# Sums of attention weights as three bf16 parts, and feed-forward matrices parked in DRAM

## The reference, cut to what matters

```python
dot = einsum('bqhd,bkhd->bhqk', q, k)
att = softmax(dot)                      # exp(dot - max) / sum over keys
out = einsum('bhqk,bkhd->bqhd', att, v) @ w_u
```

## Time and profile before

| | us |
|---|---|
| median of 3 runs (lowest, highest) | 3775.59 (3775.01, 3776.57) |
| the profiled execution | 3777.26 |
| its span in the trace | 3775.5 |
| PE busy | 3594.2 (95%) |
| DVE busy | 2860.7 (76%) |
| ACT busy | 2330.0 (62%) |
| POOL busy | 449.4 (12%) |

### The profile page before, as it was taken

The page is one execution under the profiler, slowest core; times in us unless marked ns, Lnnn a source line. Parts: engine busy times, 40 slices in busy tenths (PEclk is TensorE's granted clock), DMA queues, the critical chain, the costliest instruction groups (busy, mean ns, idle before and its releaser), DMA issues.

```text
span 3775.5 us, 66359 instructions
## 1 busy us (share of the span) xinstructions
PE 3594.2 (95%) x24697; PEld 2100.9 (56%) x24697; DVE 2860.7 (76%) x5691; ACT 2330.0 (62%) x3981; POOL 449.4 (12%) x486
## 2 busy tenths in 40 slices
PE   5999999999999977999999997899999999999999
PEld 3555555555555533665665554355555555555555
DVE  6878878778777776777777776577777878878784
ACT  4666666666666614666666653566666666666664
POOL 2000000000000002323232321000000000001000
PEclk9999999999999988999999997899999999999999
DMA  1000000000000000000000000000000000000000
GB/s 49 8 9 10 10 9 10 9 10 10 7 10 7 15 5 3 16 14 15 16 11 16 14 13 6 19 8 9 8 13 7 10 12 8 9 8 11 7 10 15
DMA packets 43641, 43.14 MB, mean 11 GB/s; under 512 B 16210, under 2 KB 30298, under 8 KB 43066
## 3 DMA queue, kind: packets, MB, share of 16 engines
q1 hardware_dynamic: 43322, 38.88, 3.6%
HBM read 36.38 MB, written 1.69 MB: 10 GB/s over the span
## 4 chain that ended last, share of the span: by engine, by line
PE 86%; DVE 7%; ACT 2%; issue 2%; SPq 1%; DMA 1%; POOL 1%; DVEq 0%; POOLq 0%
PE ps L599 83%; DVE over L1395 1%; DVE x L1578 1%; PE ps L946 1%; DVE wexp L1395 1%; PE ps L957 1%; SPq L514 1%; DMA auxQ<-mrow 1%; DVE V L1303 0%; PE ps L885 0%; DVE stats L1291 0%; PE ps L983 0%; DVE acc L1372 0%; ACT wexp L1118 0%; SPq L470 0%
## 5 line engine op out<-in xcount | busy, mean ns | idle before, releaser
L1372 DVE TENSOR_TENSOR acc<-acc,work 128x1024 f32<-128x1024 f32 (+2 forms) x1152 | 1387.6, 1205 | 62.6 <-ACT work L1103 18.6
L599 PE MATMUL ps<-work,V 128*64 128x512 f32 (+3 forms) x5376 | 1232.9, 579 | 0.0
L599 PE MATMUL ps<-Qh,Kh 64*128 64x512 f32 (+3 forms) x2688 | 864.2, 483 | 22.6 <-DMA auxQ<-mrow 9.6
L1100 ACT ACTIVATE work<-ps 128x512 f32<-128x512 f32 (+1 forms) x1344 | 790.6, 588 | 90.7 <-PE ps L599 85.5
L1395 DVE CUSTOM_DVE_ANT_0 over<-ps,over,mpart 128x512 f32<-128x512 f32 (+3 forms) x642 | 423.3, 697 | 499.2 <-PE ps L599 491.5
L1103 ACT ACTIVATE work<-ps 128x512 f32<-128x512 f32 (+1 forms) x1344 | 795.8, 592 | 0.0
L599 PEld LDWEIGHTS ps<-work,V 128*64 128x64 f32 x5376 | 448.4, 137 | 542.0 <-issue 444.5
L599 PE MATMUL ps<-Qh,Kl 64*128 64x512 f32 (+3 forms) x2688 | 732.9, 387 | 0.0
L599 PE MATMUL ps<-Ql,Kh 64*128 64x512 f32 (+3 forms) x2688 | 728.1, 384 | 0.0
L599 PE MATMUL ps<-auxQ,auxK 64*128 64x512 bf16 (+3 forms) x2688 | 720.9, 380 | 0.0
L1085 ACT ACTIVATE over<-ps 128x1024 f32<-128x1024 f32 (+1 forms) x321 | 316.1, 985 | 575.8 <-PE ps L599 575.8
(11 more groups left out here) (193 smaller groups left out, 2903.7 us busy)
## 6 DMA issues: line engine op xcount, KB each, us to landing
rden<-inverse_sums SPq DMA_DIRECT2D x186, 128.0 KB, 2.9
auxQ<-mrow SPq DMA_DIRECT2D x384, 1.0 KB
wqk<-in_wqk SPq DMA_DIRECT2D x24, 128.0 KB, 2.5
dcomp<-rden SPq DMA_DIRECT2D x186, 2.0 KB
wv<-in_wv SPq DMA_DIRECT2D x24, 64.0 KB, 2.2
inverse_sums<-rcomp SPq DMA_DIRECT2D x93, 4.0 KB, 1.3
work<-in_mlp_w SPq DMA_DIRECT2D x1, 1024.0 KB
work<-in_c_aux SPq DMA_DIRECT2D x1, 1024.0 KB, 4.9
```

What stands on the lines that cost most here:

```text
L599: return pe.matmul(o, w, m, start=start, stop=stop, skip_group_check=True)
L1100: act.activation(work[:, 2 * e, q0:CH], ps[:, b, q0:CH], ACT.Exp, scale=L.scale)\
L1372: dve.tensor_tensor(o, o, work[:, slots[two]:slots[two] + 2, q0:CH], ALU.add).then_inc(s["acc_ready"], 1)
```

## The change

- The den jobs no longer multiply `ones` with `acc` in float32. POOL's new `split` takes `acc` of a finished chunk apart: a bf16 copy (part 0), the rest, a bf16 copy of the rest (part 1), and the rest of that written as bf16 (part 2). PE sums the three parts with `onesb`, six bf16 matmuls of 512 columns for the two heads. `split` works on 128x1024, in four instructions that wait for each other. `splits_to` numbers the splits over the layers.
- In layers 0 and 2 a split stands in POOL's cycle behind `normalise`; in layer 1 at the very end of the cycle, behind `differences`. It comes in the cycle of `out_at`. The closing chunk of each layer is summed as before.
- DVE's first add into a half of `acc` waits for the split that read it, not for the den job.
- `den_at` and `op_at` move by up to two steps, and in layers 0 and 2 some Q, K and V jobs change their slots or steps.
- `wm` lies in V[1], is written to DRAM during layer 0's opening and read back in two halves, ahead of each feed-forward. ACT's first copy into V[1] waits for the write. `bT` lies in `wl2` and `obias`; `load_bias` waits for the adds of four biases.

```diff
             mt_at = ((-4, 0), (-2, 0), (1, 1), (5, 0))
-            den_at = ((2, 0), (5, 1), (8, 1), (10, 0))
-            op_at = ((4, 2), (7, 2), (10, 2), (12, 2))
+            den_at = ((3, 0), (5, 1), (8, 1), (11, 0))
+            op_at = ((6, 1), (7, 2), (10, 2), (13, 1))
         else:
             self.qk = [("K", 0), ("K", 1), ("K", 2), ("K", 3), ("Q", 0), ("Q", 1), ("Q", 2), ("Q", 3)]
-            qk_at = ((0, 1), (1, 0), (2, 1), (3, 1), (4, 1), (5, 0), (6, 1), (7, 1))
-            v_at = ((8, 1), (9, 0), (11, 1), (12, 1))
+            qk_at = ((0, 1), (1, 1), (2, 0), (3, 1), (4, 1), (5, 1), (6, 0), (7, 1))
+            v_at = ((8, 1), (9, 1), (10, 0), (11, 1))
             mt_at = ((-1, 0), (3, 0), (7, 0), (11, 0))
-            den_at = ((4, 0), (8, 0), (12, 0), (16, 0))
-            op_at = ((6, 0), (10, 0), (14, 0), (18, 0))
+            den_at = ((5, 0), (9, 0), (13, 0), (17, 0))
+            op_at = ((8, 0), (12, 0), (16, 0), (20, 0))
         self.jobs = [(g - self.G, sl, kind, c) for (g, sl), (kind, c) in zip(qk_at, self.qk)]
...
+    def splits_to(self, h, c):
+        return (NC * PAIRS - 1) * self.n + NC * h + c + 1
     def units_in(self, x):
...
         acc = sb("acc", [P, 2, 2, CH])
+        parts = [sb(f"part_{m}", [P, 2, CH], BF16) for m in range(3)]
         over = sb("over", [P, 2, CH])
...
         ones = sb("ones", [P, P])
+        onesb = sb("onesb", [P, DH], BF16)
         obias = sb("obias", [P, 6, D])
...
-        wm = sb("wm", [P, 4, FF])
+        wm = V[1][:].rearrange("p n d -> p (n d)").rearrange("p (m f) -> p m f", m=4)
+        wm_dram = nc.dram_tensor("feed_forward", [P, 4, FF], F32, kind="Internal").ap()
         b1 = sb("b1", [P, 2, NJ])
...
         bparts = [acc[0:HEADS, c // 2, c % 2, :].bitcast(BF16).rearrange("h (m q) -> h m q", m=2) for c in range(NC)]
-        bT = [wm[0:2 * TPC, p, :].rearrange("r (c q) -> r c q", q=P) for p in range(2)]
+        bT = [b[0:2 * TPC, 0:NC, :] for b in (wl2, obias)]
         over2 = wexp[:].rearrange("p (m e) f -> p m (e f)", m=2)
...
-        l2_psum, l2_ready, lo_psum, lo_used = (
-            sem(s) for s in ("l2_psum", "l2_ready", "lo_psum", "lo_used"))
+        l2_psum, l2_ready, lo_psum = (
+            sem(s) for s in ("l2_psum", "l2_ready", "lo_psum"))
...
                              "br_ready", "br_out"))
+        split_ready = sem("split_ready")
         bp_ready, fo_psum, fs_ready = sem("bp_ready"), sem("fo_psum"), sem("fs_ready")
...
                 def load_bias(h, p):
+                    sp.wait_ge(xb_ready, 4 * NC)
                     for h2 in range(2):
...
                             max_rows(0, c, 0)
+                    if L.n == 0:
+                        sp.wait_ge(weights_ready, 1)
+                        sp.dma_start(wm_dram, wm).then_inc(const_in, 16)
...
             sp.wait_ge(A[1]["x_added"], NC * PAIRS)
+            sp.wait_ge(const_in, 16 * N_CONST + 32)
+            sp.dma_start(wm[:, 0:2, :], wm_dram[:, 0:2, :]).then_inc(const_in, 16)
             attention(LAYERS[2])
+            sp.wait_ge(const_in, 16 * N_CONST + 48)
+            sp.wait_ge(A[2]["pv_done"], LAYERS[2].K * PAIRS)
+            sp.dma_start(wm[:, 2:4, :], wm_dram[:, 2:4, :]).then_inc(const_in, 16)
             for c in range(NC):
...
                     elif kind == "den":
-                        pe.wait_ge(s["acc_ready"], L.NS * h + L.sums_to[L.end[c]])
-                        for h2 in range(2):
-                            ins = mm(ps[head(h2), b, :], ones[:, 0:DH], acc[:, c % 2, h2, :], True, True)
+                        pe.wait_ge(split_ready, 4 * L.splits_to(h, c))
+                        for m in range(3):
+                            for h2 in range(2):
+                                ins = mm(ps[head(h2), b, :], onesb[:], parts[m][:, h2, :], m == 0, m == 2)
                         ins.then_inc(s["den_psum"], 1)
...
                     mm.then_inc(cT_psum, 1)
-                pe.wait_ge(const_in, 16 * N_CONST + 16)
+                pe.wait_ge(const_in, 16 * N_CONST + 32)
                 for t in range(NT):
...
                 s = F[n]
+                pe.wait_ge(const_in, 16 * N_CONST + 48 + 16 * n)
                 for c in range(NC):
...
                         act.wait_ge(s["v_psum"], NC * h + c + 1)
+                        if L.n == 0 and h == 1 and c == 0:
+                            act.wait_ge(const_in, 16 * N_CONST + 16)
                         act.activation(V[p][:, c * TPC:(c + 1) * TPC, :].rearrange("p t d -> p (t d)"), bank(b),
...
+                def split(h, c):
+                    if not L.closing(h, c):
+                        pool.wait_ge(s["acc_ready"], L.NS * h + L.sums_to[L.end[c]])
+                        at_least(pool, s["den_psum"], NC * h + c)
+                        rest = acc[:, c % 2, :, :]
+                        done = 4 * L.splits_to(h, c)
+                        pool.tensor_copy(parts[0][:], rest).then_inc(split_ready, 1)
+                        pool.wait_ge(split_ready, done - 3)
+                        pool.tensor_tensor(rest, rest, parts[0][:], ALU.subtract).then_inc(split_ready, 1)
+                        pool.wait_ge(split_ready, done - 2)
+                        pool.tensor_copy(parts[1][:], rest).then_inc(split_ready, 1)
+                        pool.wait_ge(split_ready, done - 1)
+                        pool.tensor_tensor(parts[2][:], rest, parts[1][:], ALU.subtract).then_inc(split_ready, 1)
                 def normalise(h, c):
...
                         normalise(m, c)
+                    if not L.causal:
+                        for m, c in L.due(L.out_at, x):
+                            split(m, c)
                     if L.main(x) and L.causal:
...
                             differences(m, c)
+                    if L.causal:
+                        for m, c in L.due(L.out_at, x):
+                            split(m, c)
...
                         q0 = op[1]
-                        at_least(dve, s["den_psum"], NC * n + c - 1)
+                        at_least(dve, split_ready, 4 * L.splits_to(n, c - 2))
                         dve.wait_ge(s["p_ready"], 2 * (2 * K * n + 2 * k + 2))
...
             dve.memset(ones[:], 1.0).then_inc(consts_ready, 1)
+            dve.wait_ge(consts_ready, 1)
+            dve.tensor_copy(onesb[:], ones[:, 0:DH])
             dve.wait_ge(x_in, 16)
```

## The result

The kernel after the change takes 3917.03 us (median of 4 runs, 3912.35 to 3917.36); the kernel before, on the same chip, 3776.08 us (4 runs). The ratio is 1.0367, 95% interval 1.0354 to 1.0379: 141 us slower. The prediction said 3944 us (3800 to 4080) and slower.

A forecast was written before the change was run, and what follows sets the result against it. The prediction took PE's queue, busy 95% of the span, as the bound. Its terms, -20 + 0 + 3 + 150 + 35 = +168 on 3777.3 us, gave 3945, or 3944 us as median; range 3800 to 4080.

The forecast's parts named there:

- Part 1: PE's den jobs: three bf16 passes take 0.70 us instead of 0.91 in float32; 93 jobs give -20 us.
- Part 2: POOL's split: copies of 1.1 us, subtractions of 2.4 us, with waits 7.3 us alone, bounds 4.7 and 9.9.
- Part 3: Two-input DVE adds and POOL instructions take turns; a split can cost DVE up to 7 us.
- Part 4: Layer 1: splits queued ahead of cuts delay PE by 2.9 to 7.1 us each; +150 us, bounds +75 and +226.
- Part 5: PE's clock drops after 14 long stalls in layer 1, 2.5 us lost each; +35 us, bounds 0 and +81.
- Part 6: Layers 0 and 2: turn-taking costs 0, with 0.2 us to spare at g = 12; later closing statistics +3 us.
- the long copy: Layers 0 and 2, were the split's copy 2.4 us: tops end later, 6.9 us lost per pair, +110 us.
- Part 7: Writing the feed-forward matrices to DRAM and loading them back is hidden: 0; without that cover some 5 us.
- A: Rival: all four POOL instructions at the one-input price, split 4.7 us, layer 1 costs 75; 3850 us, chance 0.12.
- B: Rival: POOL's bf16 copy costs as much as a subtraction; about 4155 us, chance 0.08.
- C: Rival: splits hidden everywhere, only the den pass is saved, so faster; 3758 us, chance 0.09.
- D: Rival: nothing measurable, stalls and savings cancel, needing about 0.7 us per split; chance 0.02.

The follow-up runs named there:

- e1: The changed kernel with layer 1's den jobs back in float32 with their old den and op tables and no splits there; 3765.34 us, ratio 0.9967.
- e5: The changed kernel with its new job tables and matrices in DRAM, but float32 den jobs in all layers and no splits; 3781.19 us, ratio 1.0010.
- e7: Against e1, each split in layers 0 and 2 makes its first bf16 copy three times, two more POOL copies; 3768.95 us, ratio 0.9979.
- e10: Against e1, each split in layers 0 and 2 makes its first bf16 copy five times, four more POOL copies; 3779.67 us, ratio 1.0002.
- e2: The changed kernel with layer 1's splits of chunks 0 to 2 queued one cycle later, behind the next slot-0 cut; 3816.28 us, ratio 1.0102.
- e3: The changed kernel with layer 1's splits cut to one copy and one subtraction, the third part left out; 3816.06 us, ratio 1.0099.
- e6: The changed kernel with unread bf16 matmuls on PE inside layer 1's stalls at g = 2 and 4; 3882.91 us, ratio 1.0279.
- e11: Against e1, both copies of each split in layers 0 and 2 become subtractions of the same shape; 3807.20 us, ratio 1.0080.
- e4: The kernel before with only the feed-forward matrices kept in DRAM, with their new waits; 3775.37 us, ratio 0.9993.
- e9: The kernel before with chunk 2's output projection in layers 0 and 2 moved to slot 1 of step 15; 3765.62 us, ratio 0.9967.

## Why the prediction was right, point by point

The sign, the place and the mechanism held; the sum of +168 measured +141. Two terms were off in opposite directions, the stalls taken 41 us too long and the clock some 13 us too cheap; that these offset each other in part was luck.

**Part 1, den jobs: right.** 0.67 us instead of the 0.70 taken: 93 x 0.24 = -22, for -20. e1 against e5 shows it in layers 0 and 2.

**Part 2, length of a split: the subtraction mis-sized.** The copy is 1.03 us (1.1 taken), the subtraction 2.12 (2.4 taken). Alone a split is 2 x 1.03 + 2 x 2.12 + 0.3 = 6.6 us, not 7.3. The fixed part of 0.17 us and 2.2 ns a column, drawn through two points, overstated the long instruction. The Trainium skill (GPSIMD Engine Reference, Engine selection) has one-input work on GpSimd near line rate and two-input work at about half of VectorE's; the trace agrees, with 1.03 and 2.12 us for 1024 columns, and 1.2 for DVE's add.

**Part 3, turns: right in the main.** A copy started under an add lasts 2.05 instead of 1.04 us, a two-input add beside a split up to 3.0 instead of 1.2, and `tops`, with an input in PSUM, keep their 0.68 to 0.75 us beside it. What the part left unsaid is that an add waits out at most one instruction, however many follow (e7, e10).

**Part 4, layer 1: right, its size less.** PE's new idle time is 109 us where 150 were summed. By place: g=2 7.04 less 0.58 before, 6.5 for 7.1; g=4 5.35 for 6.8; g=7 2.41, less 1.32 before at another matmul of the same step, for 4.0; the split of chunk 3 leaves 0.5 us ahead of `Kh,Qh` for 2.9. e1 proves that layer 1 has the whole loss, e2 that the place in the queue makes two thirds of it, e3 that the wait follows the split's length one for one. The 0.7 us by which each split was taken too long explains 20 of the 41 us. Most of the rest lies with chunks 2 and 3. For chunk 2 the prediction counted from the start of `Kh,Qh` at 1858.05 as if PE had been out of work by then, but score matmuls ran on to 1858.86:

```profile
1858.47 0.39 PE L599 MATMUL ps<-auxQ,auxK 64*128 64x512 bf16 x1
```

In the changed kernel these 0.8 us stand ahead of the wait and hide as much of it. Chunk 3's split lasts 6.9 us (1719.27 to 1726.19) where 8.0 were reckoned. None of this was tried by itself.

**Part 5, the clock: right in kind, too small.** 2.5 us for each of 14 waits was +35. Half of PE's busy time at the lower level, summed over layer 1, is 49.7 us, where the kernel before had 1.4; that is within the bound of 81. Of it 32.5 us (2.3 each) stand behind the 14 waits at g = 2 and 4, so this term was well sized, and e6 gets 34 us back with these and one more. What was left out is the third wait of each pair: 2.41 us lowered the clock too, in six of seven pairs, and cost 10.9 us, 3.2 in the pair shown and 1.5 to 1.6 in the five others. The last 6.3 us are at the layer's start, as before, and in pair 7.

**Part 6, layers 0 and 2: 0 was right, its reason only half.** The room was said to be 0.2 us at g=12 and the long copy to cost 110 us. The `tops` of slot 1 end 9.9 us behind the row start, not the 10.3 that were reckoned. e7 makes them 1.1 us later and the step at g=12 loses 0.5, so the room there was about 0.6 us, and more at the other steps, which lose nothing. e11, the long copy itself in these layers, costs 42 us. The working had charged the extra length at every add and every step, while in the runs it counts only where an add meets the longer instruction. The closing waits: 3.93 against 3.05 us at the end of layer 2, +0.9, and 3.04 against 3.03 at the end of layer 0: about +1 in all for +3.

**Part 7, matrices in DRAM: right.** e4, 0.9993 (0.9984 to 1.0001).

**Rivals.** A asked for subtractions at 1.1 us and falls with 2.12. B asked for copies at 2.4 and falls with 1.03. C is true of layers 0 and 2 and false of layer 1: e1, with splits in those two layers alone, measured 3765 for C's 3758. D has no support: the change is 3.7% slower.

## What to carry to other kernels

An engine that is busy for 12% of the time can still have no room: ask what stands behind the new work in its queue, and how soon that is due. Here 6.6 us of work, put right ahead of a cut that PE waits for, cost 109 us of stalls and nearly half as much again in clock, and the same work behind that cut gave back 101 us. Put such work where the next item of the queue is due latest. Where it takes turns with another engine, keep its single instructions short rather than few. And look for a place where the bound engine already waits for something else: in e9 a job put there cost nothing.

## What the runs showed of the hardware

- Short waits of PE in the middle of busy work lowered its clock to 0.50, though not each time. In the changed kernel each of the 14 waits of 7.04 and 5.35 us did, and six of the seven of 2.41 us; in e3 all seven of 2.04 to 2.12 us, in e2 five of the seven of 2.9 to 3.3 us. The waits of 1.32 or 1.33 us in e1, one in each pair, did not. The cost did not follow the length of the wait: 2.4 us on average behind 7.04, 2.2 behind 5.35, and 1.8 behind the six of 2.41 us. Matmuls with no reader, put into the wait, kept the clock at 1.00 (e6).
- DVE and POOL took turns by whole instructions: an add of 1.2 us that came just after a 2.12 us subtraction began lasted 2.97 us, and the subtraction behind it 2.99 (e11). Beside a copy of 1.04 us such an add lasted 1.6 to 1.9 us. So a subtraction beside an add held DVE up more than a copy did, and adding copies to a split cost little (e7, e10) where lengthening them cost much (e11).
